# Row copies moved from SP's to ScalarE's queue, one wait placed later, and an FFN add cut into four

## The chip, the cores and the metric

One Trainium2 chip, all 8 cores. The batch has 16 sequences; each core computes two of them, one after the other, with no traffic between cores. The metric is the device time of the slowest core in microseconds.

## What is computed

One pre-norm transformer layer in float32, for x of 16 x 2048 x 2048:

```python
h = layernorm(x)
q = rmsnorm(h @ Wqa, q_a_ln_w) @ Wqb          # 1536 latent, 16 heads x (128 + 64)
ckv = h @ Wkva                                # 512 latent + 64 rope
kv = rmsnorm(ckv[:, :512], kv_a_ln_w) @ Wkvb  # 16 heads x (128 key + 128 value)
q_pe, k_pe = rope(q[..., 128:]), rope(ckv[:, 512:])
attn = softmax(causal((q_nope @ k_nope.T + q_pe @ k_pe.T) * 192 ** -0.5))
x = x + (attn @ v) @ Wo
x = x + (layernorm(x) @ sum_r factors[r]) / sqrt(8) + bias
```

## The kernel before

Instructions are put by hand into five lists, one for each engine (TensorE, VectorE, ScalarE, SP, POOL), and each engine works through its own list in order. `E(engine, fn, waits, inc)` adds one; it stands still until all its semaphores have their values, and everything behind it on that engine's list stands with it. A DMA is issued by the engine in whose list it is. SP, ScalarE and POOL issue DMAs here.

Each sequence runs through these stages: layernorm and latent projections (L294 to L467), the rope part of all queries (L480 to L532), the 16 heads of attention (L806 to L979), the output projection with the first residual (L999 to L1070), and the FFN (L1085 to L1171). The FFN matrix is the sum of 8 factors; POOL builds it in DRAM with 128 accumulating loads and 16 stores while the first sequence's heads run (`emit_f_build`, L210).

**Between two heads.** After head h's softmax sums (L914) the reciprocals are transposed and copied as two rows into `invflat` (L937, L939); TensorE spreads them over all partitions (L949, L953), VectorE scales the output (L961), ScalarE issues its store (L966). Then comes `prep(h+1)`: the query projection L635, whose four groups increment `c_bn`, the keys L652, the values L672 and a transpose of the rope queries L691, with evictions on ScalarE (L642, L659) and VectorE (L680, L697). `emit_mhat(h+1)` follows, a chain of small steps on TensorE, VectorE and ScalarE (L737 to L799) that bounds each query's largest score. `augstats(h+1)` turns the bound into two rows (`sb_st`, L824) and copies them with two small DMAs into rows 64 and 65 of `QpeT_aug` (L826, L829), semaphore `c_aug`.

**At the start of head h's loop** stands `head_dmas(h+1)`, the weights of the next head. SP loads the query weights into `stage_w` (L591) once `c_whf` and `c_bn` say that the old ones are used; ScalarE scales them in 12 activations (L596). Then SP loads the key part (L601), ScalarE scales it in 4 (L606), SP the value part (L611), ScalarE in 4 (L616), and SP loads the rope queries (L621). Only behind these 20 activations stand head h's own exponentials on ScalarE (L882). TensorE waits for `c_aug` at L845, then for each of 16 key tiles writes score chunks (L866 with the 128 nope rows, L871 with the 66 rows that include the copied two) into three PSUM banks in turn. A bank is free when L882 has read it. VectorE masks the diagonal (L889); L902 multiplies with the values, L914 sums.

Head 15 has no `head_dmas` before it, and the weights of head 0 are loaded ahead of the loop, so in each sequence there are 15 gaps with these loads.

**An FFN tile** (16 per sequence): SP loads `r1f` (L1103), ScalarE normalizes it (L1108), TensorE transposes (L1125) and ScalarE evicts (L1131), then come 8 bias matmuls and 64 of L1155, in the order `kb` outside and four column blocks of 512 inside, so the blocks are done one matmul apart. VectorE adds the residual over all 2048 columns (L1164), SP stores the tile (L1168). On SP's list the load of the next tile stands behind this store.

Of the kernel before, what the change touches and what calls it, by code (L numbers as in the profile page):

```python
# [85 lines left out]
def build_nc():  # L86
# [159 lines left out]
    def _emit_seq(sq):  # L246
# [564 lines left out]
        def augstats(h, mh_mark):  # L811
            hb = h % 2
            E("vector", lambda e, hb=hb: e.tensor_copy(
                out=stat_h[:, 0:16], in_=neg_mh[:, hb * 16:(hb + 1) * 16]),
              waits=[mh_mark, (c_statT, c_statT.n)], inc=c_v)
            E("vector", lambda e, hb=hb: e.tensor_sub(
                out=stat_h[:, 16:32], in0=neg_mh[:, hb * 16:(hb + 1) * 16],
                in1=stat_h[:, 0:16]),
              waits=[(c_v, c_v.n)], inc=c_stat)
            E("tensor", lambda e: e.matmul(  # L820
                out=psB[0:32, 1536:1664], lhsT=stat_h[:], rhs=ident[:],
                start=True, stop=True),
              waits=[(c_stat, c_stat.n)] + list(bank3_marks), inc=c_statT)
            E("vector", lambda e: e.tensor_copy(out=sb_st[:], in_=psB[0:32, 1536:1664]),  # L824
              waits=[(c_statT, c_statT.n), (c_aug, c_aug.n)], inc=c_statT_ev)
            E("sync", lambda e, hb=hb: e.dma_start(  # L826
                out=QpeT_aug[hb][64:65, :], in_=sb_st[0:16, :]),
              waits=[(c_statT_ev, c_statT_ev.n)], inc=c_aug, inc_amt=16)
            E("sync", lambda e, hb=hb: e.dma_start(  # L829
                out=QpeT_aug[hb][65:66, :], in_=sb_st[16:32, :]),  # L830
              inc=c_aug, inc_amt=16)
            return (c_statT_ev, c_statT_ev.n)
# [7 lines left out]
        for h in range(NH):  # L840
# [1 line left out]
            if h + 1 < NH:  # L842
                head_dmas(h + 1)

            p.wait("tensor", [(c_aug, c_aug.n)])  # L845
            av_head_base = c_av.n
            binit = [(c_pt, c_pt.n)]
            if bcast_ev_mark[0]:
# [6 lines left out]
            for kt in range(NT):  # L855
                qmin = kt * 128
                pto = 2048 * (kt % 2)
                ch_list = _chunks(qmin, S)
                pt_of_chunk = []
                for (q0, wd) in ch_list:  # L860
                    bsel = st_ctr % 3
                    st_ctr += 1
                    boff = 512 * bsel
                    stw = list(st_last[bsel]) if isinstance(st_last[bsel], list) \
                        else [st_last[bsel]]
                    E("tensor", lambda e, hb=hb, kt=kt, q0=q0, wd=wd, boff=boff: e.matmul(  # L866
                        out=psB[:, boff:boff + wd],
                        lhsT=KnT[hb][:, kt * 128:(kt + 1) * 128],
                        rhs=QnT[hb][:, q0:q0 + wd], start=True, stop=False),
                      waits=stw)  # L870
                    E("tensor", lambda e, hb=hb, kt=kt, q0=q0, wd=wd, boff=boff: e.matmul(  # L871
                        out=psB[:, boff:boff + wd],
                        lhsT=kpeT_aug[:, kt * 128:(kt + 1) * 128],
                        rhs=QpeT_aug[hb][:, q0:q0 + wd], start=False, stop=True),
                      inc=c_st)
                    ew = [(c_st, c_st.n)]
                    if q0 == qmin:
                        if kt >= 2:
                            ew.append((c_av, av_abs[kt - 2]))
                        elif av_head_base > 0:  # L880
                            ew.append((c_av, av_head_base - (1 if kt == 0 else 0)))
                    E("scalar", lambda e, q0=q0, wd=wd, boff=boff, pto=pto: e.activation(  # L882
                        out=ptpool[:, pto + q0:pto + q0 + wd],
                        in_=psB[:, boff:boff + wd], func=AF.Exp),
                      waits=ew, inc=c_pt)
                    st_last[bsel] = (c_pt, c_pt.n)
                    pt_of_chunk.append(c_pt.n)
                    if q0 == qmin:
                        E("vector", lambda e, qmin=qmin, pto=pto: e.tensor_tensor(  # L889
                            out=ptpool[:, pto + qmin:pto + qmin + 128],  # L890
                            in0=ptpool[:, pto + qmin:pto + qmin + 128],
                            in1=maskT[:], op=ALU.mult),
                          waits=[(c_pt, c_pt.n)], inc=c_ptm)
                for i2, (q0, wd) in enumerate(ch_list):
                    avw = [(c_pt, pt_of_chunk[i2])]
                    if i2 == 0:
                        avw.append((c_ptm, c_ptm.n))
                        if kt == 0:
                            avw += pm_ev
                            if h > 0 or sq > 0:  # L900
                                avw.append((c_ot_ev, c_ot_ev.n))
                    E("tensor", lambda e, hb=hb, kt=kt, q0=q0, wd=wd, pto=pto: e.matmul(  # L902
                        out=psA[:, q0:q0 + wd],
                        lhsT=Vh[hb][:, kt * 128:(kt + 1) * 128],
                        rhs=ptpool[:, pto + q0:pto + q0 + wd],
                        start=(kt == 0),
                        stop=(kt == min(NT - 1, (q0 + wd - 1) // 128))),
                      waits=avw, inc=c_av)
                av_abs.append(c_av.n)
                for qt in range(kt, NT):  # L910
                    sgw = []
                    if kt == 0 and qt == 0:
                        sgw = list(sg_first)
                    E("tensor", lambda e, kt=kt, qt=qt, pto=pto: e.matmul(  # L914
                        out=psB[:, 1536 + qt:1537 + qt],
                        lhsT=ptpool[:, pto + qt * 128:pto + (qt + 1) * 128],
                        rhs=ones_col[:],
                        start=(kt == 0 and qt == 0),
                        stop=(kt == NT - 1 and qt == NT - 1)),
                      waits=sgw,  # L920
                      inc=(c_sg if qt == NT - 1 else None))
# [12 lines left out]
            E("vector", lambda e: e.tensor_sub(out=invTlo[:], in0=invT[:], in1=invThi[:]),  # L934
              waits=[(c_v, c_v.n)], inc=c_v)
            iv_mark = (c_v, c_v.n)
            E("sync", lambda e: e.dma_start(out=invflat[:, 0:2048], in_=invThi[:]),  # L937
              waits=[iv_mark, (c_aug, c_aug.n)], inc=c_aug, inc_amt=16)
            E("sync", lambda e: e.dma_start(out=invflat[:, 2048:4096], in_=invTlo[:]),  # L939
              inc=c_aug, inc_amt=16)  # L940
            flat_mark = (c_aug, c_aug.n)
            bank3_marks = [(c_statT_ev, c_statT_ev.n), rec_mark, (c_v, iv_mark[1])]
# [153 lines left out]
        for tt in range(NT):  # L1096
# [16 lines left out]
            for g in range(4):  # L1113
                gs = 512 * (g % 2)
                tw = [(c_ln2, c_ln2.n)]
                if g < 2:
                    if tt < 2:
                        tw += slot_wo[sl]
                    else:
                        tw.append((c_outv, outv_at[tt - 2]))  # L1120
                else:
                    tw.append((c_trF_ev, c_trF_ev.n - 1))
                for j in range(4):
                    blk = g * 4 + j
                    E("tensor", lambda e, blk=blk, gs=gs, j=j, bi=bi, ps=ps: e.matmul(  # L1125
                        out=ps[:, gs + j * 128:gs + (j + 1) * 128],
                        lhsT=ln2_bf[bi][:, blk * 128:(blk + 1) * 128], rhs=ident[:],
                        start=(j == 0), stop=(j == 3)),
                      waits=(tw if j == 0 else []),
                      inc=(c_trF if j == 3 else None))  # L1130
                E("scalar", lambda e, g=g, gs=gs, bi=bi, ps=ps: e.activation(  # L1131
                    out=ln2T[bi][:, g * 512:(g + 1) * 512], in_=ps[:, gs:gs + 512],
                    func=AF.Copy),
                  waits=[(c_trF, c_trF.n)], inc=c_trF_ev)
# [8 lines left out]
            for cci in range(4):  # L1143
# [6 lines left out]
                    out=ps[:, cci * 512:(cci + 1) * 512], lhsT=ones1[:],  # L1150
                    rhs=bias_hl[:, D + cci * 512:D + (cci + 1) * 512],
                    start=False, stop=False))
            for kb in range(16):
                for cci in range(4):
                    E("tensor", lambda e, kb=kb, cci=cci, bi=bi, ps=ps: e.matmul(  # L1155
# [1 line left out]
                        lhsT=ln2T[bi][:, kb * 128:(kb + 1) * 128],  # L1157
                        rhs=f_bf[:, kb * 2048 + cci * 512:kb * 2048 + (cci + 1) * 512],
                        start=False, stop=(kb == 15)),
                      inc=(c_ffn if (kb == 15 and cci == 3) else None))  # L1160
            ow = [(c_ffn, c_ffn.n)]
            if tt >= 2:
                ow.append((c_out[bi], out_at[tt - 2]))
            E("vector", lambda e, bi=bi, ri=ri, ps=ps: e.tensor_add(  # L1164
                out=out_sb[bi][:], in0=ps[:, :], in1=r1f[ri][:]),
              waits=ow, inc=c_outv)
            outv_at[tt] = c_outv.n
            E("sync", lambda e, sq=sq, tt=tt, bi=bi: e.dma_start(  # L1168
                out=x_out[sq, tt * 128:(tt + 1) * 128, :], in_=out_sb[bi][:]),
# [93 lines left out]
```

## Time and profile before

| | us |
|---|---|
| timed runs | 7183.54 and 7230.93, median 7207.23 |
| the profiled execution | 7173.46 |
| its span (core 1, the slowest of 8) | 7171.9 |
| busy in it: TensorE, ScalarE, VectorE | 4214.1 (59%), 1663.6 (23%), 1223.6 (17%) |

The chain that ended last runs 54% through TensorE, 13% through DMAs, 12% through ScalarE and 8% through VectorE. A profile's start times are microseconds from the start of the span. SPq and ACTq are the instruction queues of SP and ScalarE, where DMA issues are shown; the duration there is that of the issue and not of the transfer. PEclk is the granted TensorE clock as a share of 2.4 GHz.

### The profile page before, as it was taken

The page shows a single profiled execution, that of the slowest core. Times are in us where ns is not written, and L with a number is a line of the kernel's source. Part 1 is how long each engine was busy: PE and PEld are TensorE (multiplying, and loading weights), DVE is VectorE, ACT ScalarE, POOL GpSimd, SP SyncE. Part 2 cuts the span into 40 slices and gives each one's busy share as a digit, 9 for nine tenths or more (in the row PEclk, how much of TensorE's full clock was granted, in tenths as well). Part 3 has the DMA queues.
Part 4 walks back from the last instruction along what each step waited for, and adds up shares of the span by engine and source line. Part 5 has one row for each costly group of instructions (what it writes and reads, how often), then busy time and mean ns, then how long its engine had stood idle before and what let it go on. Part 6 is the DMA issues. An engine that isn't in the chain of part 4 may idle for free.

```text
span 7171.9 us, 67365 instructions; the slowest of 8 cores (7113.9 to 7171.9 us)
## 1 busy us (share of the span) xinstructions
PE 4214.1 (59%) x23712; PEld 1907.6 (27%) x23712; DVE 1223.6 (17%) x2068; ACT 1663.6 (23%) x3289; POOL 209.6 (3%) x300
## 2 busy tenths in 40 slices
PE   3663655545555664946646646556565655557656
PEld 1331322222222221422212323222222222223222
DVE  1221321111212120100002213121111212101000
ACT  2331222222232321311113320322222232223111
POOL 0000000000000000000000000000000000000000
PEclk8776866666676676967767767767676666778777
DMA  4102167676650005331140121000000000054111
GB/s 85 36 30 22 37 132 139 135 140 133 133 105 20 17 16 134 145 106 59 59 95 30 36 19 42 17 24 16 21 16 21 15 21 17 23 169 155 59 63 61
DMA packets 290396, 467.00 MB, mean 65 GB/s; under 512 B 140321, under 2 KB 226593, under 8 KB 253217
## 3 DMA queue, kind: packets, MB, share of 16 engines
q0 software_dynamic: 88704, 199.77, 15.3%
q1 hardware_dynamic: 187554, 204.19, 9.1%
q10 hardware_dynamic: 13824, 58.73, 2.0%
q8 instruction: 213, 3.49, 0.2%
q14 instruction: 101, 0.83, 0.0%
HBM read 401.82 MB, written 100.66 MB: 70 GB/s over the span
## 4 chain that ended last, share of the span: by engine, by line
PE 54%; DMA 13%; ACT 12%; DVE 8%; issue 7%; another core or an unknown queue 3%; SPq 2%; DVEq 0%; ACTq 0%; POOL 0%; POOLq 0%
PE psA L902 6%; PE psA L635 6%; PE psA L377 5%; PE psB L1155 4%; PE psA L1155 4%; DMA stage_w_u<-wkvb 3%; PE psA L1028 3%; PE psB L866 3%; PE psB L1028 3%; PE psB L871 3%; ACT ptpool L882 3%; DMA r1f_u<-r_s 3%; DMA stage_w_u<-wqb 3%; PE psA L503 2%
## 5 line engine op out<-in xcount | busy, mean ns | idle before, releaser
L866 PE MATMUL psB<-QnT_u,KnT_u 128*128 128x512 bf16 (+3 forms) x1280 | 506.8, 406 | 597.1 <-ACT ptpool L882 467.2
L882 ACT ACTIVATE ptpool<-psB 128x512 bf16<-128x512 f32 (+3 forms) x1280 | 630.3, 531 | 745.4 <-PE psB L871 736.2
L902 PE MATMUL psA<-ptpool,Vh_u 128*128 128x512 bf16 (+3 forms) x1280 | 451.8, 400 | 282.5 <-DVE ptpool L889 223.6
L871 PE MATMUL psB<-QpeTa_u,kpeT_aug 66*128 66x512 bf16 (+3 forms) x1280 | 529.9, 414 | 0.0
L635 PE MATMUL psA<-qa_nT,wqbnh_u 128*128 128x512 bf16 x1536 | 411.4, 437 | 187.1 <-DVE otst_u L961 150.3
L377 PE MATMUL psA<-wa_bf,ln1T_u 128*128 128x512 bf16 x1536 | 473.9, 422 | 61.2 <-DVE ln1T_u L350 47.4
L889 DVE TENSOR_TENSOR ptpool<-ptpool,maskT 128x128 bf16<-128x128 bf16 x512 | 115.2, 225 | 1903.8 <-ACT ptpool L882 1903.8
L1028 PE MATMUL psA<-wo_bf_u,OT_wo_u 128*128 128x512 bf16 x1024 | 228.6, 385 | 183.2 <-DMA wo_bf_u<-wo 183.2
L866 PEld LDWEIGHTS psB<-QnT_u,KnT_u 128*128 128x128 bf16 x1280 | 134.3, 106 | 720.6 <-issue 682.0
L902 PEld LDWEIGHTS psA<-ptpool,Vh_u 128*128 128x128 bf16 x1280 | 131.0, 102 | 680.6 <-issue 664.6
L1108 ACT ACTIVATE ln2bf_u<-r1f_u,stat_ln 128x2048 bf16<-128x2048 f32 x32 | 67.0, 2093 | 954.4 <-DMA r1f_u<-r_s 954.4
L635 PEld LDWEIGHTS psA<-qa_nT,wqbnh_u 128*128 128x128 bf16 x1536 | 165.5, 109 | 445.0 <-issue 314.1
L503 PE MATMUL psA<-wqbpe_bf,qa_nT 128*128 128x512 bf16 x768 | 170.6, 386 | 164.8 <-ACT wqbpe_bf L487 164.8
L642 ACT ACTIVATE QnT_u<-psA 128x512 bf16<-128x512 f32 x128 | 76.4, 597 | 815.4 <-PE psA L635 815.4
L1155 PE MATMUL psB<-f_bf_u,ln2T_u 128*128 128x512 bf16 x1024 | 257.1, 418 | 0.0
L1155 PE MATMUL psA<-f_bf_u,ln2T_u 128*128 128x512 bf16 x1024 | 256.7, 417 | 0.0
L344 PE MATMUL psB<-ident,ln_bf_u 128*128 128x128 bf16 x512 | 69.8, 303 | 284.1 <-ACT ln_bf_u L328 262.0
L377 PE MATMUL psB<-wa_bf,ln1T_u 128*128 128x512 bf16 (+1 forms) x1024 | 229.1, 308 | 0.0
L596 ACT ACTIVATE wqbnh_u<-stage_w_u,qlnw 128x128 bf16<-128x128 f32 x384 | 115.5, 387 | 478.3 <-DMA stage_w_u<-wqb 478.3
L1028 PE MATMUL psB<-wo_bf_u,OT_wo_u 128*128 128x512 bf16 x1024 | 223.6, 379 | 0.0
L914 PEld LDWEIGHTS psB<-ones_col,ptpool 128*128 128x128 bf16 x4352 | 193.8, 100 | 83.0 <-issue 43.3
L914 PE MATMUL psB<-ones_col,ptpool 128*128 128x1 bf16 x4352 | 191.0, 166 | 0.0
(152 smaller groups left out, 4645.3 us busy)
## 6 DMA issues: line engine op xcount, KB each, us to landing
acc_f<-fac POOLq DMA_DIRECT2D x128, 1024.0 KB, 8.5
xs_u<-x SPq DMA_DIRECT2D x32, 1024.0 KB, 5.1
xre_u<-x SPq DMA_DIRECT2D x32, 1024.0 KB, 5.8
r_s<-r1sb_u ACTq DMA_DIRECT2D x32, 1024.0 KB, 3.9
r1f_u<-r_s SPq DMA_DIRECT2D x32, 1024.0 KB, 6.7
out<-outsb_u SPq DMA_DIRECT2D x32, 1024.0 KB, 4.7
stage_w_u<-wqb SPq DMA_DIRECT2D x32, 768.0 KB, 5.1
stage_w_u<-wkvb SPq DMA_DIRECT2D x64, 256.0 KB, 3.1
```

The source lines that it names most:

```text
L377: E("tensor", lambda e, ti=ti, kb=kb, dst=dst, do=do, wdt=wdt, woff=woff: e.matmul(out=dst[:, do:do + wdt], lhsT=ln1T[ti][:, kb * 128:(kb ...
L503: E("tensor", lambda e, tt=tt, kb=kb, cci=cci, base=base: e.matmul(out=psA[:, base + cci * 512:base + (cci + 1) * 512], lhsT=qa_v()[:, kb, ...
L596: E("scalar", lambda e, kb=kb, hb=hb: e.mul(out=wqbn_h[hb][:, kb * 128:(kb + 1) * 128], in_=stage_w[:, kb * 128:(kb + 1) * 128], mul=qlnw[ ...
L635: E("tensor", lambda e, kb=kb, cci=cci, bps=bps, boff=boff: e.matmul(out=bps[:, boff:boff + 512], lhsT=wqbn_h[hb][:, kb * 128:(kb + 1) * 128],
L866: E("tensor", lambda e, hb=hb, kt=kt, q0=q0, wd=wd, boff=boff: e.matmul(out=psB[:, boff:boff + wd], lhsT=KnT[hb][:, kt * 128:(kt + 1) * 12 ...
L871: E("tensor", lambda e, hb=hb, kt=kt, q0=q0, wd=wd, boff=boff: e.matmul(out=psB[:, boff:boff + wd], lhsT=kpeT_aug[:, kt * 128:(kt + 1) * 128],
L882: E("scalar", lambda e, q0=q0, wd=wd, boff=boff, pto=pto: e.activation(out=ptpool[:, pto + q0:pto + q0 + wd], in_=psB[:, boff:boff + wd], ...
L889: E("vector", lambda e, qmin=qmin, pto=pto: e.tensor_tensor(out=ptpool[:, pto + qmin:pto + qmin + 128], in0=ptpool[:, pto + qmin:pto + qmi ...
L902: E("tensor", lambda e, hb=hb, kt=kt, q0=q0, wd=wd, pto=pto: e.matmul(out=psA[:, q0:q0 + wd], lhsT=Vh[hb][:, kt * 128:(kt + 1) * 128], rhs ...
L914: E("tensor", lambda e, kt=kt, qt=qt, pto=pto: e.matmul(out=psB[:, 1536 + qt:1537 + qt], lhsT=ptpool[:, pto + qt * 128:pto + (qt + 1) * 12 ...
L1028: E("tensor", lambda e, tt=tt, hh=hh, cci=cci, ps=ps: e.matmul(out=ps[:, cci * 512:(cci + 1) * 512], lhsT=OT_wo[:, hh * 2048 + tt * 128:hh ...
L1155: E("tensor", lambda e, kb=kb, cci=cci, bi=bi, ps=ps: e.matmul(out=ps[:, cci * 512:(cci + 1) * 512], lhsT=ln2T[bi][:, kb * 128:(kb + 1) * ...
```

## The change

Three edits. The two row copies of `augstats` and the two of `invflat` are issued by ScalarE instead of SP, at the places that their calls have in the program; the standing wait of TensorE for `c_aug` is removed and put on the first L871 of the head, behind the first L866. The FFN add is cut into four adds of 512 columns, each of which waits for its own column block; `c_outv` still rises to one final value that the store and the `r1f` load wait for, and the first two parts have marks of their own, for which the transposes two tiles later wait.

```diff
-            E("sync", lambda e, hb=hb: e.dma_start(
+            E("scalar", lambda e, hb=hb: e.dma_start(
                 out=QpeT_aug[hb][64:65, :], in_=sb_st[0:16, :]),
               waits=[(c_statT_ev, c_statT_ev.n)], inc=c_aug, inc_amt=16)
-            E("sync", lambda e, hb=hb: e.dma_start(
+            E("scalar", lambda e, hb=hb: e.dma_start(
                 out=QpeT_aug[hb][65:66, :], in_=sb_st[16:32, :]),
               inc=c_aug, inc_amt=16)
...
-            p.wait("tensor", [(c_aug, c_aug.n)])
+            aug_mark = (c_aug, c_aug.n)
...
                         rhs=QpeT_aug[hb][:, q0:q0 + wd], start=False, stop=True),
+                      waits=([aug_mark] if kt == 0 and q0 == qmin else []),
                       inc=c_st)
...
-            E("sync", lambda e: e.dma_start(out=invflat[:, 0:2048], in_=invThi[:]),
+            E("scalar", lambda e: e.dma_start(out=invflat[:, 0:2048], in_=invThi[:]),
               waits=[iv_mark, (c_aug, c_aug.n)], inc=c_aug, inc_amt=16)
-            E("sync", lambda e: e.dma_start(out=invflat[:, 2048:4096], in_=invTlo[:]),
+            E("scalar", lambda e: e.dma_start(out=invflat[:, 2048:4096], in_=invTlo[:]),
               inc=c_aug, inc_amt=16)
...
-                        tw.append((c_outv, outv_at[tt - 2]))
+                        tw.append((c_outv, outv_at[(tt - 2, g)]))
...
-                      inc=(c_ffn if (kb == 15 and cci == 3) else None))
-            ow = [(c_ffn, c_ffn.n)]
-            if tt >= 2:
-                ow.append((c_out[bi], out_at[tt - 2]))
-            E("vector", lambda e, bi=bi, ri=ri, ps=ps: e.tensor_add(
-                out=out_sb[bi][:], in0=ps[:, :], in1=r1f[ri][:]),
-              waits=ow, inc=c_outv)
+                      inc=(c_ffn if kb == 15 else None))
+                    if kb == 15:
+                        ffn_marks[cci] = c_ffn.n
+            ov0 = [(c_out[bi], out_at[tt - 2])] if tt >= 2 else []
+            for cci in range(4):
+                E("vector", lambda e, bi=bi, ri=ri, cci=cci, ps=ps: e.tensor_add(
+                    out=out_sb[bi][:, cci * 512:(cci + 1) * 512],
+                    in0=ps[:, cci * 512:(cci + 1) * 512],
+                    in1=r1f[ri][:, cci * 512:(cci + 1) * 512]),
+                  waits=[(c_ffn, ffn_marks[cci])] + (ov0 if cci == 0 else []),
+                  inc=c_outv, inc_amt=(1 if cci < 3 else 2))
+                if cci < 2:
+                    outv_at[(tt, cci)] = c_outv.n
```

## Rows read from the trace of the kernel before

**Rows 1.** The page's first line: span and cores.
```profile
span 7171.9 us, 67365 instructions; the slowest of 8 cores (7113.9 to 7171.9 us)
```

**Rows 2.** Waits, whole span: who waited for whom, us in total, times, longest.
```profile
ACT wqbnh_u L596 <- DMA stage_w_u<-wqb: 478.3, 32, 96.8
...
PE psB L866 <- ACT ptpool L882: 467.2, 30, 25.3
...
PE psB L866 <- DMA QpeTa_u<-sb_st: 129.9, 32, 8.5
```

**Rows 3.** Chain of waits through one gap of sequence 1: start, us, what.
```profile
5166.00 0.50 SPq L826
...
5166.55 0.57 SPq L829
...
5167.27 5.12 DMA stage_w_u<-wqb
...
5172.48 3.62 ACT wqbnh_u L596 x12
...
5184.96 0.49 ACT ptpool L882
...
5185.58 0.58 PE psB L866
```

**Rows 4.** Chain, whole span: `prep` of neighbouring heads, two of each sequence.
```profile
1542.85 13.05 PE psA L635 x48
...
1673.01 12.83 PE psA L635 x48
...
5126.02 13.46 PE psA L635 x48
...
5242.14 13.43 PE psA L635 x48
```

**Rows 5.** Waits of SP's instruction queue, whole span.
```profile
SPq L71 <- DVE sb_st L824: 1605.5, 32, 54.5
```

**Rows 6.** Issue of L966 and L829, ns min/median/max; landings of L591, us.
```profile
L966 ACTq DMA_DIRECT2D ot_s<-otst_u x32: 326/326/327, 917.1 to 6264.0; - x32
...
L829 SPq DMA_DIRECT2D QpeTa_u<-sb_st x32: 562/575/746, 841.0 to 6205.9; - x32
...
DMA to landing us min/median/max: 4.6/5.1/11.2
```

**Rows 7.** Waits in 787:2740 (sequence 0's heads), then in 4423:6300 (sequence 1's).
```profile
ACT wqbnh_u L596 <- DMA stage_w_u<-wqb: 159.8, 15, 14.6
...
ACT wqbnh_u L596 <- DMA stage_w_u<-wqb: 125.2, 15, 8.7
```

**Rows 8.** Timeline of ScalarE: a gap of sequence 0, then that of rows 3.
```profile
1592.44 3.61 ACT L596 ACTIVATE wqbnh_u<-stage_w_u,qlnw 128x128 bf16<-128x128 f32 x12 [12.05 <-DMA stage_w_u<-wqb]
...
5163.73 0.22 ACT L795 ACTIVATE neg_mh_u<-neg_mh_u 128x16 f32<-128x16 f32 x1
```

**Rows 9.** Windows: us, busy (x) of PE, PEld, DVE, ACT, POOL, PEclk, DMA share, GB/s.
```profile
1583.00:1612.50 29.50, 3.73 (x8) 0.88 (x8) 0.22 (x1) 7.61 (x23) 2.60 (x3) 0.50 0.90 169
...
5185.60:5190.00 4.40, 4.34 (x26) 1.78 (x27) 0.17 (x1) 1.67 (x4) 0.00 (x0) 0.50 0.00 0
5190.00:5215.00 25.00, 21.58 (x183) 9.85 (x181) 2.02 (x9) 13.55 (x28) 0.00 (x0) 0.98 0.01 1
...
6216.00:6240.00 24.00, 20.28 (x178) 9.28 (x177) 1.98 (x9) 12.79 (x27) 0.00 (x0) 1.00 0.00 1
```

**Rows 10.** FFN tile end: timeline, chain (two); four 512-column casts in the attention.
```profile
3353.18 2.75 PE L1155 MATMUL psB<-f_bf_u,ln2T_u 128*128 128x512 bf16 x12
...
3356.11 2.30 DVE outsb_u L1164
...
3358.97 6.96 DMA r1f_u<-r_s
...
5147.22 2.47 DVE L697 CAST QpeTa_u<-psA 64x512 bf16<-64x512 f32 x4
```

## What I predict

> **What bounds the kernel now.** I read the spans of the cores first, then the list of who waited for whom, then the chain of waits and the timelines of one gap between two heads, and last the end of one FFN tile. The cores lie between 7113.9 and 7171.9 us [rows 1], so no core is a special case, and what every head pays is paid on all of them.
>
> The waits [rows 2] show where ScalarE and TensorE stand still in the attention: ScalarE 478.3 us for the load of the next head's query weights, TensorE 467.2 us for ScalarE's exponentials at L882. The second follows from the first. `head_dmas(h+1)` puts 20 scaling activations ahead of head h's exponentials on ScalarE, and TensorE may write only three score chunks before it needs a bank that L882 empties.
>
> The chain of the gap [rows 3] has the order. Once `sb_st` is written, SP issues the two row copies of `augstats` (5166.00, 5166.55), and only then, at 5167.27, the query weight load, which lands after 5.12 us. The 12 scalings follow, then two more loads and eight scalings, then the first exponential at 5184.96. What the weight load needs had been there for long: its old weights' last reader L635 began at 5126.02 and took 13.46 us [rows 4], so it ended at 5139.5, 28 us before the issue. SP's own waits [rows 5] say the same: 1605.5 us, 32 times, for `sb_st` of L824, behind which the load is queued. What sets each gap is SP's program order. It is no shortage of bandwidth.
>
> In the FFN the same kind of chain runs through SP [rows 10]: the add of 2048 columns (2.30 us), the store, then the next `r1f` load of 6.96 us, while TensorE waits.
>
> **The change part by part.**
>
> *The two copies of `augstats` go to ScalarE's queue.* SP then has nothing between the last `qpesl` load and L591, and the weight load starts at about 5139.5. It has 27 us before ScalarE wants it; its longest time to landing is 11.2 us [rows 6]. So it is hidden whole, under `prep` and `emit_mhat`. Were that cover gone, the cost of before would be back, not more. ScalarE instead waits for `sb_st` and issues both copies. Behind them on ScalarE are the 12 scalings, which before began later still, and behind those only SP (L601) waits.
>
> The sum is made from ScalarE's idle time before L596: 159.8 us for the 15 gaps of sequence 0, 125.2 us for the 15 of sequence 1 [rows 7], together 285.0. (The rest of the 478.3 is the first load of each sequence, which isn't moved.) What remains of each gap: ScalarE ends L795 at 5163.95 [rows 8], and SP's second copy ended at 5166.55 + 0.57 = 5167.12. If ScalarE issues as SP did, the scalings start 3.2 us after L795. 30 x 3.2 = 97. Saved: 285 - 97 = 188 us.
>
> ScalarE's issue of such a row copy is not in the trace. Its own issue of `ot_s` takes 0.326 us every time, SP's second row copy 0.562 to 0.746 [rows 6]. Two at 0.326 instead of SP's 1.07 in sum would give 0.5 us more per gap (+14 us), two at 0.746 would take 0.4 (-12). I take SP's own, the same kind of copy.
>
> The Trainium skill (DMA: Bandwidth & Descriptors, "Issuing engines are not separate DMA queues") says that starting DMAs from several engines only saves the time that a sequencer needs to start them. Read as a rule for this edit it speaks against the sum; the rival "only the issue" below is what it would make of it. The trace does not bear that reading out: by rows 5 a semaphore wait holds SP's queue, not issue work.
>
> *A cost in sequence 0.* The factor sums of POOL (128 transfers of 1 MB) keep the DMA engines 0.90 busy in the gap at 1583 [rows 9], and their length does not depend on the heads. A head there takes 1673.01 - 1542.85 = 130.2 us, one of sequence 1 takes 5242.14 - 5126.02 = 116.1 [rows 4]. Of the 14.1 between them 12.05 - 8.53 = 3.5 are the load that gets hidden [rows 3, 8]. 10.6 stay for each head that runs beside the sums. The heads there become some 80 us shorter in sum, so 0.7 of a head more falls into them: 7 us lost. Bounds: 0, and half of what sequence 0 gains, (159.8 - 48) / 2 = 56.
>
> *The wait for the copies goes from ahead of L866 to the first L871.* One score matmul of some 0.5 us (0.58 in [rows 3]) runs ahead. It matters only where exponentials follow at once, at head 15 of each sequence: 2 x 0.5 = 1 us. In the other 30 heads the wait of [rows 2], 129.9 / 32 = 4.1 us, lies beside the ScalarE chain: the copies are issued at 5166.00 and 5166.55, and the first exponential starts at 5184.96. 0 us.
>
> *The `invflat` copies go to ScalarE.* SP is free at that point, and ScalarE has no work left in the head, since the last sums (L914) and the transposition of the reciprocals stand between its last exponential and the copies. Same wait, same transfer: 0 us. Behind them on ScalarE stand only the `ot_s` store and the next QnT evictions, which wait for later work anyway. Bounds: the same 0.5 and 0.4 us as above, 32 times, +16 and -13.
>
> *The FFN add in four parts.* Four operations of 512 columns from PSUM, all released, took 2.47 us in one row [rows 10], a start every 0.60. They may begin when column block 0 is done, three matmuls before the last one; 12 matmuls take 2.75 us at that place, so three take 0.65. The end comes 2.30 - (2.47 - 0.65) = 0.48 us sooner, and with it store, `r1f` load and all behind: 32 x 0.48 = 15 us. If each part costs its 0.69 us in turn, 2.76 us in sum, 0.19 us is left, 6 us. The finer marks for L1125 two tiles later are worth 0: that add has been done for a whole tile. TensorE's four increments instead of one: 0, no row prices an increment.
>
> The Trainium skill (VectorE: DVE Perf Modes, "The TRN2 errata — SBUF-src ops pay a fixed extra latency per instruction") has it that many small tiles each pay the fixed time. By that this part is worth the 6 us, and the forecast is 9 us more. The row of four supports the shorter sum.
>
> **Sum.** 188 - 7 + 1 + 0 + 15 = 197 us. The profiled execution took 7173.46 us (span 7171.9), so 6976 for one like it. The median of the timed runs is 7207.23, 34 us above it; the same saving there gives 7207 - 197 = 7010 us, 2.7% less.
>
> **The rivals.**
>
> *Only the issue.* SP's order did not hold the load, and moving two copies saves what SP spent between the first copy and the load, 5167.27 - 5166.00 = 1.27 us. 30 x 1.27 = 38, with 15 from the FFN 53: 7154 us. For it: L591 has waits of its own, `c_whf` and `c_bn`. Against it: both are met 28 us earlier [rows 4]. Chance 5%.
>
> *The factor sums eat half of sequence 0.* The moved load meets saturated DMA engines, and the loads that remain get slower by what it no longer waits for. 188 - 56 + 1 + 15 = 148: 7059 us. For it: 169 GB/s in the gap at 1583 [rows 9]. Against it: the loads of one head still run one after the other. Chance 13%.
>
> *The TensorE clock, slower than before.* After the gap TensorE runs 4.4 us at a granted 0.50 (1.2 GHz), then 25 us at 0.98 (2.4 GHz) [rows 9]. If the shorter gap made the clock rise later, each us of the warm stretch's work would take two. It decides from 197 / 32 = 6.2 us per head, a rise 12 us later than now. With the whole 21.58 busy us at 1.2 GHz a head costs 21 us more, 32 x 21 - 197 = +475: 7682 us. For it: before the gap, too, TensorE has little work, and the clock falls to 0.50 there. Against it: head 15 has no gap at all, and its stretch from 6216 is at 1.00 [rows 9]. Chance 3%.
>
> The forecast has 79%.
>
> **How the numbers follow.** 2% of 7207 is 144 us, about what a measurement of this kernel can tell from no change; the line is 7063. The forecast's own bounds: most, 188 + 14 + 1 + 16 + 15 = 234, 6973 us; least, 188 - 12 - 7 - 13 + 6 = 162, 7045 us. The timed runs lie 24 us to either side of their median. The range takes the most and 8 us of scatter, 6965, and reaches up over the second rival with its scatter, 7059 + 24 = 7083, and 12 us more for a gap that keeps 0.4 us more than costed (30 x 0.4): 7095. "Only the issue" and the clock are left out. Faster by over 2%: the forecast but for a tail of 0.05, and half of the second rival, 0.81. Within 2%: that tail, the other half, and the first rival, 0.15 after rounding. Slower: 0.04, the clock and what I don't see.
>
> **What the profile after would show.** ScalarE's wait for the query weights is gone in the gaps, or some 3 us each under another name; L591 is issued near the end of L635's last group; the two copies stand on ScalarE's queue at 0.3 to 0.75 us each; a head of sequence 1 lasts 111 us instead of 116.1; the last part of L1164 ends 1.9 us after the last matmul instead of 2.4; the warm stretch is at 0.98 as before. I am wrong if L591 still starts behind L824, if the copies take over 3 us each on ScalarE, or if a head of sequence 1 lasts as long as before.

## The result, and the profile after

| | us |
|---|---|
| changed kernel, 11 timed runs | 6970.25 to 7229.65, median 7102.42 |
| kernel before, 10 timed runs | 7155.66 to 7410.15, median 7228.97 |
| ratio of the times | 0.972, 95% interval 0.967 to 0.977 |
| profiled execution, before and after | 7173.46 and 6989.14 |

The medians hold slow runs of both kernels, in which the cores of one die or of both show a lower granted TensorE clock; the ratio leaves these out, and the five other timed runs of the changed kernel lie between 6970.25 and 6993.07. The change made the kernel faster, by 2.8%; the forecast was 7010 against 7207, a ratio of 0.973. The two profiled executions differ by 184.3 us.

First the page of the changed kernel (span and cores; compare [rows 1]) and its waits, in the columns of [rows 2]:

```profile
span 6987.5 us, 67557 instructions; the slowest of 8 cores (6935.0 to 6987.5 us)
...
PE psB L866 <- ACT ptpool L883: 345.2, 30, 19.3
...
ACT wqbnh_u L596 <- DMA stage_w_u<-wqb: 193.7, 2, 96.9
...
ACT wkvbvh_u L616 <- DMA stage_w_u<-wkvb: 149.1, 32, 8.7
...
ACT wkvbkh_u L606 <- DMA stage_w_u<-wkvb: 126.4, 32, 9.3
ACT wqbnh_u L596 <- issue: 101.2, 30, 4.0
...
PE psB L871 <- DMA QpeTa_u<-sb_st: 95.6, 32, 8.4
```

The same two waits for the key and value parts in the kernel before:

```profile
ACT wkvbvh_u L616 <- DMA stage_w_u<-wkvb: 134.1, 32, 8.4
...
ACT wkvbkh_u L606 <- DMA stage_w_u<-wkvb: 108.7, 32, 5.3
```

Of ScalarE's 478.3 us for the query weights only the two first loads are left. In the 30 gaps it now stands 101.2 us under the name "issue", which is the wait for `sb_st` and the two issues. The waits for the key and value parts have grown, by 17.7 and 15.0 us. TensorE waits 122 us less for the exponentials (L882 before, L883 now).

SP's own waits come next (L71 is the line of the helper that waits). Before, 1605.5 us stood here for `sb_st` [rows 5]; now SP stands at L591 until L635 is done, as the load needs:

```profile
SPq L71 <- PE psA L635: 1987.8, 30, 76.4
...
SPq L71 <- ACT wqbnh_u L596: 956.8, 32, 32.8
```

One gap of sequence 1, the chain, to be laid beside [rows 3]. Between the second copy and the scalings there is no DMA any more:

```profile
5032.81 0.23 ACT neg_mh_u L795
...
5035.09 0.53 ACTq L826
...
5035.64 0.61 ACTq L829
...
5036.36 3.62 ACT wqbnh_u L596 x12
...
5040.04 2.74 DMA stage_w_u<-wkvb
...
5044.21 3.29 DMA stage_w_u<-wkvb
...
5048.86 0.49 ACT ptpool L883
```

And SP's timeline of the same gap: L591 is issued at 5008.38, 28 us ahead of the first scaling.

```profile
5008.38 0.37 SPq L591 DMA_DIRECT2D stage_w_u<-wqb  x1
5040.04 0.37 SPq L601 DMA_DIRECT2D stage_w_u<-wkvb  x1
```

### The profile page after: what moved, and what is told of

Same layout as the page of the kernel before. It is cut to its first block, busy times and chain, and to the rows that moved or that the text cites. A ratio compares the mean times of both kernels' runs of the same rounds, so it can differ in the third digit from the quotient of the medians.

```text
span 6987.5 us, 67557 instructions; the slowest of 8 cores (6935.0 to 6987.5 us)
## 1 busy us (share of the span) xinstructions
PE 4194.3 (60%) x23712; PEld 1902.5 (27%) x23712; DVE 1230.0 (18%) x2164; ACT 1663.3 (24%) x3289; POOL 209.6 (3%) x300
## 4 chain that ended last, share of the span: by engine, by line
PE 55%; ACT 13%; DMA 12%; DVE 8%; issue 7%; another core or an unknown queue 3%; ACTq 1%; SPq 1%; DVEq 0%; POOL 0%; POOLq 0%
PE psA L903 6%; PE psA L635 6%; PE psA L377 6%; DMA stage_w_u<-wkvb 4%; PE psB L1157 4%; PE psA L1157 4%; PE psA L1029 3%; PE psB L1029 3%; PE psB L866 3%; ACT ptpool L883 3%; PE psB L871 3%; DMA r1f_u<-r_s 3%; PE psA L503 2%; PE psB L377 2%
## 5 line engine op out<-in xcount | busy, mean ns | idle before, releaser
L883 ACT ACTIVATE ptpool<-psB 128x512 bf16<-128x512 f32 (+3 forms) x1280 | 629.8, 531 | 734.0 <-PE psB L871 724.3
L866 PE MATMUL psB<-QnT_u,KnT_u 128*128 128x512 bf16 (+3 forms) x1280 | 503.2, 404 | 345.4 <-ACT ptpool L883 345.2
L871 PE MATMUL psB<-QpeTa_u,kpeT_aug 66*128 66x512 bf16 (+3 forms) x1280 | 523.1, 409 | 95.6 <-DMA QpeTa_u<-sb_st 95.6
L635 PE MATMUL psA<-qa_nT,wqbnh_u 128*128 128x512 bf16 x1536 | 407.0, 433 | 187.8 <-DVE otst_u L962 150.3
L1109 ACT ACTIVATE ln2bf_u<-r1f_u,stat_ln 128x2048 bf16<-128x2048 f32 x32 | 67.0, 2093 | 940.5 <-DMA r1f_u<-r_s 940.5
L635 PEld LDWEIGHTS psA<-qa_nT,wqbnh_u 128*128 128x128 bf16 x1536 | 164.2, 108 | 442.4 <-issue 309.2
L866 PEld LDWEIGHTS psB<-QnT_u,KnT_u 128*128 128x128 bf16 x1280 | 132.1, 104 | 463.9 <-issue 419.5
L1157 PE MATMUL psB<-f_bf_u,ln2T_u 128*128 128x512 bf16 x1024 | 255.2, 416 | 0.0
L1157 PE MATMUL psA<-f_bf_u,ln2T_u 128*128 128x512 bf16 x1024 | 253.6, 414 | 0.0
L385 ACT ACTIVATE ptpool<-psB 128x512 bf16<-128x512 f32 x32 | 19.1, 597 | 702.3 <-PE psB L377 702.3
```

The lines of the kernel that those rows point to most:

```text
L635: E("tensor", lambda e, kb=kb, cci=cci, bps=bps, boff=boff: e.matmul(out=bps[:, boff:boff + 512], lhsT=wqbn_h[hb][:, kb * 128:(kb + 1) * 128],
```

## What all eight cores say

The slowest core is not the same one in every execution, and the cores of one execution differ by some 50 us, so I took the same stretches on all 8 cores of each profiled execution. A head sequence is the time from the first to the last issue of L621 in it; the FFN is the time from the first to the last store issue of it, 15 tiles. Means over the cores, in us:

| | heads, seq. 0 | heads, seq. 1 | ScalarE at L596, seq. 0 / 1 | at L606 | at L616 | TensorE for `invflat` |
|---|---|---|---|---|---|---|
| before | 1769.8 | 1671.4 | 156.4 / 124.5 | 57.5 / 45.2 | 81.7 / 49.5 | 76.8 / 52.7 |
| changed | 1686.3 | 1596.1 | 50.8 / 50.4 | 66.9 / 44.9 | 87.3 / 49.6 | 82.3 / 53.1 |
| e1, `augstats` copies only | 1676.0 | 1589.9 | 52.0 / 50.0 | 64.2 / 44.8 | 84.0 / 49.4 | 83.4 / 52.7 |
| e2, all but these | 1775.9 | 1675.2 | 153.5 / 125.6 | 58.0 / 44.8 | 81.1 / 49.4 | 75.0 / 53.5 |
| e3, SP's list reordered | 1642.1 | 1543.0 | 0 / 0 | 77.5 / 45.0 | 87.8 / 49.2 | 79.8 / 52.7 |
| e4, four copies on ScalarE | 1697.7 | 1610.3 | 72.6 / 70.8 | 61.7 / 44.7 | 81.8 / 49.4 | 80.8 / 52.9 |
| e5, before without the sums | 1681.9 | 1671.6 | 128.6 / 124.8 | 47.6 / 45.3 | 50.9 / 49.6 | 54.3 / 52.7 |
| e6, changed without the sums | 1598.8 | 1597.2 | 51.4 / 50.4 | 46.5 / 44.5 | 50.2 / 49.1 | 54.4 / 53.1 |

(e3: the head lengths are means of cores 0 to 3 alone, at a granted clock of 0.730 to 0.736; cores 4 to 7 had 0.713 to 0.717.) Kernels with the same waits still differ by 6 to 10 us in a head sequence, as the changed kernel and e1 do. Nothing smaller than that is read from the first two columns.

## Experiments

**e1: the `augstats` copies alone.** The kernel before, with this edit only:

```diff
-            E("sync", lambda e, hb=hb: e.dma_start(
+            E("scalar", lambda e, hb=hb: e.dma_start(
                 out=QpeT_aug[hb][64:65, :], in_=sb_st[0:16, :]),
...
-            E("sync", lambda e, hb=hb: e.dma_start(
+            E("scalar", lambda e, hb=hb: e.dma_start(
                 out=QpeT_aug[hb][65:66, :], in_=sb_st[16:32, :]),
```

> The kernel before with one edit: the two sb_st row copies of augstats go from SP's to ScalarE's list. My theory (SP's order held the next query weight load behind the wait for sb_st): all of the attention's gain is here. By the two traces the heads of the changed kernel are 84 us shorter in sequence 0 (mean of the cores) and 75 in sequence 1: -159 to -170 us against before, ratio about 0.977; a head of sequence 1 takes 110 to 111 us, an FFN tile is unchanged. Rival (the moved wait for the copies or the invflat copies give a good part of it): less than -130 us, and a head of sequence 1 over 112 us.

Ratio 0.976 (0.968 to 0.984). The heads are 94 and 82 us shorter than before, no less than in the changed kernel; the FFN is as before (532 and 534 us). The whole gain of the attention is in these two edits.

**e2: everything else.** The changed kernel with the two lines put back.

> The changed kernel with the two sb_st row copies of augstats put back on SP's list; the invflat copies stay on ScalarE, the wait stays at L871 and the add stays in four. My theory: a head of sequence 1 is 115 to 116 us again, L591 is issued behind the sb_st copies again, the FFN tiles stay 0.5 us shorter: -15 to -17 us against before, ratio 0.998, which the timing will call the same. Rival (the other edits carry part of the attention's gain): -50 us or more, heads of sequence 1 under 114 us.

Ratio 0.997 (0.992 to 1.003). SP's list holds the load again, at the same distance behind the second copy as in [rows 3] (timeline of SP, core 0):

```profile
4985.94 0.51 SPq L826 DMA_DIRECT2D QpeTa_u<-sb_st  x1
4986.49 0.58 SPq L829 DMA_DIRECT2D QpeTa_u<-sb_st  x1
4987.23 0.47 SPq L591 DMA_DIRECT2D stage_w_u<-wqb  x1
```

The heads are 6 and 4 us longer than before, within what equal kernels differ by: the wait placed later and the `invflat` copies on ScalarE gave nothing that can be seen. The FFN took 522.4 and 522.7 us instead of 531.8 and 533.1.

**e3: the order without the other engine.** The kernel before; `load_wqb` holds L591 alone and is called ahead of `augstats`:

```diff
+                if h + 2 < NH:
+                    load_wqb(h + 2)
                 st_ev_mark = augstats(h + 1, mh_ready)
```

> The kernel before with SP's list alone reordered: the query weight load L591 of the next head stands ahead of the two sb_st row copies, which stay on SP. Everything else is as before. My theory (order on SP, not which engine issues): the load starts about 28 us sooner, and ScalarE's scalings follow L795 at once, without the 3.3 us that they wait for sb_st and the issue in the changed kernel. 285 us of ScalarE's wait go, less some 20 us of slower loads beside the factor sums: -250 to -270 us against before, ratio 0.964, more than the whole change. Rival (the gain comes from ScalarE's queue, or from issue time saved on SP): 0 to -40 us.

Ratio 0.970 (0.962 to 0.979); the fastest run took 6929.81 us, below every run of the changed kernel. On cores 0 to 3 the heads are 133 and 129 us shorter than those of before on the same cores (1774.7 and 1672.1), and 43 and 54 shorter than in the changed kernel there (1684.8 and 1597.0). That is 262 us in sum, inside the 250 to 270 that were expected, and the spans of these four cores are 262 us shorter too (means 6884 and 7146). The timed ratio, expected at 0.964, came out nearer to 1; its interval reaches down to 0.962. This kernel has not one DMA more on ScalarE. ScalarE's timeline, core 0 (L797, L598 and L886 are L795, L596 and L882 of before):

```profile
5070.85 0.22 ACT L797 ACTIVATE neg_mh_u<-neg_mh_u 128x16 f32<-128x16 f32 x1 [0.37 <-ACT neg_mh_u L794]
5070.97 3.62 ACT L598 ACTIVATE wqbnh_u<-stage_w_u,qlnw 128x128 bf16<-128x128 f32 x12
...
5083.19 1.54 ACT L886 ACTIVATE ptpool<-psB 128x512 bf16<-128x512 f32 x3
```

The scalings start with the end of L797, where [rows 8] and [rows 3] have 8.53 us between them. So the place in SP's list was the cause, and the changed kernel pays 3.4 us per gap, 101 us in 30 gaps, for having taken the other way out; 43 + 54 = 97 of them show in the heads.

**e4: twice the copies on ScalarE.** The changed kernel with two more copies behind the two:

```diff
+            for i in range(2):
+                E("scalar", lambda e, i=i: e.dma_start(
+                    out=spare[i][:], in_=sb_st[16 * i:16 * i + 16, :]),
+                  inc=c_dup, inc_amt=16)
```

> The changed kernel with two more copies of the same sb_st rows, to spare rows that nobody reads, behind the two on ScalarE. Doubles ScalarE's issue work in each gap. My theory (what remains of the gap ahead of the scalings, 3.3 us, is the wait for sb_st plus two issues of 0.53 and 0.61 us, all of it on the path): 30 x 1.2 = 36 us slower than the changed kernel, so about 0.977 of before; ScalarE L596 waits 4.5 us instead of 3.3. Rival (issue work on ScalarE overlaps with its next instructions): within 10 us of the changed kernel, 0.973.

Ratio 0.976 (0.969 to 0.982). ScalarE's timeline, core 0 (L828, L831 and L598 are L826, L829 and L596):

```profile
5051.18 0.53 ACTq L828 DMA_DIRECT2D QpeTa_u<-sb_st  x1
5051.74 0.61 ACTq L831 DMA_DIRECT2D QpeTa_u<-sb_st  x1
5052.38 1.25 ACTq L835 DMA_DIRECT2D spare_u<-sb_st  x2
5053.73 3.63 ACT L598 ACTIVATE wqbnh_u<-stage_w_u,qlnw 128x128 bf16<-128x128 f32 x12 [4.68 <-issue]
```

The scalings wait for all four issues; the wait grew by 21.8 and 20.4 us. The heads grew by 11 and 14, where 36 in sum were expected. The issue time is on the path, but only some 60% of the wait shows in the length, and with 6 to 10 us between equal kernels this run can't say whether the difference is real.

**e5 and e6: without the factor sums.** The kernels before and after with one factor loaded instead of eight (the FFN's matrix is then not the sum):

```diff
-            for r in range(1, 8):
+            for r in range(1, 1):
```

> The kernel before without the factor sums: only factor 0 is loaded, 7 of 8 loads of L218 are left out, so the FFN matrix is not the sum. My theory: the heads of sequence 0 are as long as those of sequence 1 (115.4 instead of 122 us): about -95 us against before, ratio 0.987. Rival (sequence 0 is slower for another reason): no change.

> The changed kernel without the factor sums (only factor 0 is loaded, as in the run beside it). My theory: both sequences gain the same 75 us from the change, with 15 from the FFN 165 us less than the kernel before without the sums, and ScalarE's waits L606 and L616 in sequence 0 fall from about 67 and 87 us to 45 and 50. So beside the sums the hidden load saved more (105 us of ScalarE's wait in sequence 0 against 74 in sequence 1) but gave some 20 of it back in slower key, value and invflat loads. Rival (the loads got slower because the query load's early issue disturbs them, sums or not): L606 and L616 stay above 60 and 80 us in sequence 0.

Ratios to the kernel before 0.987 (0.979 to 0.995) and 0.961 (0.956 to 0.967), 0.0255 apart: 184 us of the 7222 that the kernel before took beside them in the median, much as with the sums. (The two intervals make that some 70 us to either side, so the reading goes by the table.) In e6 sequence 0 is as long as sequence 1, in e5 all but 10 us, and the waits at L606 and L616 are down to 46.5 and 50.2. Beside the sums the change removed 156.4 - 50.8 = 105.6 us of ScalarE's wait at L596 in sequence 0, and 9.4 + 5.6 + 5.5 = 20.5 came back at L606, L616 and `invflat`. 85 is left, and the heads got 83.5 shorter. Without the sums it removed 77.2 and gave nothing back; the heads got 83.1 shorter. So what is given back needs the sums; the early load alone does not cause it.

**e7 and e11: the weights ahead of the bound.** The changed kernel, with `head_dmas` moved:

```diff
+                if h + 2 < NH:
+                    head_dmas(h + 2)
                 mh_ready = emit_mhat(h + 1, prep_marks)
...
-            if h + 1 < NH:
-                head_dmas(h + 1)
```

> The changed kernel with the whole of head_dmas(h+1), three loads and 20 scalings, ahead of emit_mhat(h) in the program, where ScalarE stands idle for 20 us. My theory: ScalarE has no load to wait for between L795 and the exponentials; the gap ends when the row copies have landed (about 1.8 us after their issue). A head of sequence 1 falls from 109.8 to about 99 us, as head 15 (99 us, no loads ahead of it) has it now: 321 us, and some 50 more in sequence 0: 6989 - 370 = 6620 us, ratio 0.923. Rival (the scalings delay L792 and the chain of the bound by as much): under 100 us less than the changed kernel.

Four runs, 6640.60 to 6699.69 us; the kernel before took 7156.63 to 7297.67 beside them. The profiled execution took 6663.21, 326 less than the changed kernel's. Its slowest cores are 0 to 3, at a granted clock of 0.743 to 0.744; cores 4 to 7, at 0.751 to 0.756, have spans 381 us shorter than in the changed kernel (means 6597 and 6978), which is what the expectation's 370 says. All scalings and their loads lie in ScalarE's idle time, ahead of L792. The gap is now the chain below (core 0; L869 is the L871 of the changed kernel). TensorE starts 1.9 us behind the second copy's issue (4865.77), ScalarE's first exponential 0.7 us later; in the changed kernel 13.2 us lay between that issue (5035.64) and the first exponential (5048.86):

```profile
4864.85 0.29 DVE sb_st L824
...
4865.21 0.53 ACTq L826
...
4865.77 1.78 DMA QpeTa_u<-sb_st
...
4867.69 0.59 PE psB L869
```

L621 has another place in this kernel, so I measured it from the first to the last store of `ot_s`, with 14 such gaps between: 1548.9 and 1480.9 us against 1730.7 and 1640.7 in the changed kernel (means of the cores), 182 and 160 less, 13.0 and 11.4 a gap. For sequence 1 I had expected 10.7. The same kernel was run again as e11:

> The kernel of e7 once more, with more rounds: 6660 us against 7180 of before, ratio 0.923 by my theory (0.915 to 0.930).

Six runs from 6607.25 to 6999.44; only the fastest had a granted clock over 0.75 on all eight cores, so no ratio came of it. Fastest run against fastest run is 6607.25 to 7175.10 here, 0.921, and 6640.60 to 7156.63 in e7, 0.928. The two sets do not contradict 0.923, and they do not confirm it to better than a per cent.

**e8 and e9: the `r1f` load a tile ahead.** As e7, and in the FFN:

```diff
+            if tt == 0:
+                r1_load(0)
+            if tt + 1 < NT:
+                r1_load(tt + 1)
```

in place of the load of tile tt at this point, so that a load no longer stands behind the store of the tile before it.

> As the run before, and in the FFN the r1f load of the next tile stands ahead of the wait for this tile's add on SP's list. My theory: the load and L1109 lie under the matmuls, a tile takes 23 us (15.5 of matmuls, 3.4 of bias, 3.6 of transposes) instead of 34.9, 30 x 12 = 360 us less: 6260 us, ratio 0.873. Rival (the clock falls or the loads collide with the stores): 100 to 250 us less than the run before.

> The kernel of e8 once more, with more rounds, beside the next two: again 0.865 of before by my theory (range 0.855 to 0.875), an FFN tile of about 20.5 us.

Ratios 0.865 (0.856 to 0.875) and 0.861 (0.856 to 0.865). An FFN tile of e9 takes 20.5 us, less than the 23 that I had expected. Windows of one tile, the slowest core of the changed kernel and of e9 (columns of [rows 9]):

```profile
3345.20:3380.10 34.90, 21.02 (x88) 8.93 (x88) 2.48 (x4) 4.26 (x5) 0.00 (x0) 0.74 0.18 66
```

```profile
6103.60:6124.10 20.50, 18.73 (x89) 8.27 (x88) 2.52 (x5) 4.26 (x5) 0.00 (x0) 0.92 0.29 102
```

The same 88 or 89 matmuls (a record is missing in one) take 2.3 us less as well, since TensorE no longer pauses and the granted clock in the tile rose from 0.74 to 0.92. That is where my 23 us were too many: I had taken bias matmuls and transposes at the slower level. The 8 bias matmuls are busy 4.96 us in the first window and 2.98 in the second, the 16 transposes 2.08 and 1.38.

**e10: e9 with the add in one piece.**

> The kernel of e9 with the FFN add in one piece of 2048 columns again. My theory (the split was worth its 0.5 us a tile only because the add stood on the chain that released the r1f load; with the load a tile ahead nothing waits for the add): the same time as e9 within 5 us, an FFN tile the same within 0.1 us. Rival (the split helps by itself, since PSUM halves come free sooner): 15 us more than e9.

Ratio 0.861 (0.855 to 0.866), the same. The last 14 stores of sequence 1 span 266.2 us on core 0 in e9 and in e10 alike, 13 tiles of 20.5 us. VectorE's timeline in e10 (L1177 is the add, L1166 the matmul) shows the whole add once in each tile:

```profile
6120.28 2.29 DVE L1177 TENSOR_TENSOR outsb_u<-psA,r1f_u 128x2048 f32<-128x2048 f32 x1 [18.18 <-PE psA L1166]
6140.75 2.29 DVE L1177 TENSOR_TENSOR outsb_u<-psB,r1f_u 128x2048 f32<-128x2048 f32 x1 [18.18 <-PE psB L1166]
```

e9 is the best version found: 6199.39 us in the median of its seven runs, 14% less than before.

## Why the prediction was right, step by step

**The query load behind `sb_st`.** Right, and by the mechanism named. e1 has the gain, e2 hasn't, e3 gets it without moving anything to ScalarE. The rival "only the issue" falls with e3 (133 + 129 us where it gives 38). The cover held too: the load is issued 28 us ahead, and the longest one took 11.9 us to land. A head of sequence 1, from one L635 to the next, takes 110.2 us in the mean of all cores where it took 115.1 (5.1 less were forecast, 5.0 came).

**188 us from ScalarE's wait.** The term was right, 8 us too large: before 280.9 us (mean of the cores), after 101.2, so 180. On the profiled cores 285.0 and 101.2, so 184. What was left per gap is 3.37 us where I had 3.2. ScalarE's issues took 0.526 and 0.613 us in the median, near SP's 0.503 and 0.575; the bound from `ot_s` (0.326) was of another kind of transfer.

**7 us lost beside the factor sums.** Too small. The table gives 20.5, and the head lengths say that 83.5 of 105.6 arrived. e1 and e4, with the load as early, gave back 15.6 and 8.3 in the same three columns, so the size is known no better than 8 to 21 us. The step that failed is the count of 0.7 more heads beside the sums as the only cost, 7 us of it. The count itself came out: from one L635 to the next on core 1, the third to the tenth head of sequence 0 took 122 us or more before and the eleventh 115.9; in the changed kernel the third to the eleventh take 114.9 to 126.4 and the twelfth 110.0. But its 80 us are worked out nowhere (the prediction's own wait for sequence 0 gives 159.8 - 48 = 112), and it left out that key, value and `invflat` loads wait longer. The rival that put the loss at 56 had that in it, and was wrong in size. e6 shows that the loss needs the sums; how the early load and the sums together make the other loads slower was not tried.

**1 us for the wait, 0 for `invflat`.** e2 finds nothing for both, with the 6 to 10 us that it can tell. The `augstats` copies are waited for 95.6 us instead of 129.9, beside the ScalarE chain as before.

**15 us for the add in four.** Four adds took 2.48 us, where the row of casts had 2.47, and the end came 1.9 us after the last matmul as forecast: chain at the end of a tile of the changed kernel, beside [rows 10].

```profile
3020.00 3.04 PE psA L1157 x14
...
3023.09 1.89 DVE outsb_u L1167 x3
...
3025.04 0.34 SPq L1176
...
3025.69 6.49 DMA r1f_u<-r_s
```

By the Trainium skill (VectorE: DVE Perf Modes, "The TRN2 errata — SBUF-src ops pay a fixed extra latency per instruction") many small tiles each pay a fixed time. Little of that shows here: the four adds take 0.68 us each but start 0.60 us apart, so in sum they are 0.18 us longer than the one of 2.30, and the end came 0.5 us sooner, not 0.2. Over 15 tiles and 8 cores the FFN went from 531.8 to 523.6 us in sequence 0 and from 533.1 to 518.9 in sequence 1, 22 in sum, somewhat more than the 15. On the profiled cores TensorE's waits for the normalization (L1108, now L1109) fell by 412.4 - 400.8 = 11.6, and the matmuls (L1155, now L1157) were busy 513.8 - 508.8 = 5.0 less. On all cores TensorE was busy 8.3 us less in these 30 tiles, at a granted clock of 0.734 and 0.740 where it was 0.722 and 0.721, and with 30 x 0.48 = 14 for the earlier end that makes the 22; in e2 it is 5.8 + 14 = 20, and 19.8 were measured. Why the clock was higher was not tried. e10 shows that the part has worth only while the add stands between the matmuls and the next load.

**The clock rival.** It did not come. The warm stretch is at 0.98 as before. In the gap shown it begins 8.5 us after TensorE's restart (5049.48) and not 4.4 [rows 9]:

```profile
5053.40:5058.00 4.60, 4.60 (x27) 1.90 (x26) 0.23 (x1) 2.28 (x4) 0.00 (x0) 0.50 0.00 0
5058.00:5083.00 25.00, 20.98 (x174) 9.43 (x171) 2.15 (x10) 13.12 (x28) 0.00 (x0) 0.98 0.00 1
```

One gap of each kernel does not tell, though. Over the 30 gaps of all eight cores the granted clock rose 4.2 to 10.9 us after the first exponential before, 7.7 in the mean, and 4.2 to 10.7 us after it in the changed kernel, 7.9 in the mean; both gaps shown are ordinary ones of the same scatter. The sum says the same: the heads of sequence 1 got 75.3 us shorter for 74.1 us of wait, and the mean clock of the slowest core's execution rose from 0.724 to 0.733.

**The sum.** 197 forecast; 83.5 + 75.3 + 22 = 181 from the stretches of all cores, 184 between the profiled executions, 0.028 of 7229 = 202 by the ratio of the timed runs, whose interval is +-35 us. ScalarE's wait gave 8 us less than costed, the loss beside the sums was 13 us larger and the FFN's gain 7 us larger, so part of the agreement is luck.

## What to carry to other kernels

An engine that issues DMAs works through a list: a load whose inputs have long been ready waits behind every copy ahead of it that is not. Look in the issuing queue's own waits for what it stood at before a load that others waited for, and move the load ahead (e3) before moving the late copy to another engine. Ask the same of the compute engine that uses the load: ScalarE had 20 idle us just ahead of the gap, and putting the loads and scalings there (e7) was worth another 326 us between the profiled executions after the change's 184, and 381 on the four cores at the higher clock. An operation that ends a tile is worth cutting up only while something waits for its end (e10).

## What the runs showed of the hardware

A row copy of 4 KB (16 partitions to one) holds ScalarE for 0.53 to 0.61 us at its issue in the median, 1.6 to 1.8 times the 0.336 us of a 512 KB store, and its next activation starts only behind it (3.37 us per gap, 4.7 with four copies). The copy lands 1.7 to 1.8 us after its issue in the median, and up to 7.7 us after it in heads that run beside the factor sums; the 768 KB load of the query weights lands after 5.1 us in the median and up to 11.9 beside them. In the FFN, with a pause of 12 us filled, the granted clock over the tile was 0.92 instead of 0.74 and the same matmuls were busy 2.3 us less.
